# Decoder of a Trainium2 megakernel: the rows of maxima are sent by DMAs that ScalarE issues, not SyncE

## The reference

```python
qkv = x @ Wi.T + bi
scores = einsum('bhqd,bhkd->bhqk', q, k) / sqrt(HD) + mask      # causal + alibi
attn = softmax(scores, axis=-1)
out = einsum('bhqk,bhkd->bhqd', attn, v)
x = x + out @ Wo.T + bo
x = x + gelu(layer_norm(x) @ W1.T + b1) @ W2.T + b2
```

## Time and profile before

| what | value |
|---|---|
| runs, median (lowest, highest) | 3368.85 us (3360.95, 3370.55), n = 3 |
| the profiled execution, its own time | 3376.56 us |
| its span; granted clock | 3374.8 us; 0.841 |
| decoder's second pass, first to last exponential | about 158 to 1608 us of the span |
| DMA issues of rows of maxima | 192, all by SyncE, 4 KB each |

### The profile page before, as it was taken

One profiled execution on the slowest core, in us unless ns is written; L12 is line 12 of the kernel. 1 busy time (PEld: TensorE's weight loads), 2 busy tenths in 40 slices (PEclk: granted clock), 3 DMA queues, 4 the chain that ended last, 5 costly groups with the idle time before them and its releaser, 6 DMA issues. The chain is left out here.

```text
span 3374.8 us, 38611 instructions
## 1 busy us (share of the span) xinstructions
PE 2632.2 (78%) x12745; PEld 1113.1 (33%) x12745; DVE 1938.5 (57%) x4374; ACT 1426.5 (42%) x2500; POOL 580.1 (17%) x595
## 2 busy tenths in 40 slices
PE   6489898979979798998676898862566695888847
PEld 4233333333424233332232344330222342222225
DVE  2376666656757565774255723348999524766243
ACT  2155555545646554666243032333333242355510
POOL 1100111110101111100055001004878201000000
PEclk7599988988979897999678998875888797798978
DMA  2211212120211212110100000000000002110010
GB/s 69 87 64 42 81 39 77 48 87 30 77 55 68 73 39 77 38 57 24 40 1 6 1 0 23 0 13 0 0 0 0 25 0 87 40 38 31 14 76 13
DMA packets 64218, 129.88 MB, mean 38 GB/s; under 512 B 18698, under 2 KB 34442, under 8 KB 60334
## 3 DMA queue, kind: packets, MB, share of 16 engines
q1 hardware_dynamic: 64020, 127.42, 10.7%
HBM read 92.30 MB, written 34.08 MB: 37 GB/s over the span
## 5 line engine op out<-in xcount | busy, mean ns | idle before, releaser
L1432 ACT ACTIVATE sb_prob<-ps 128x512 f32<-128x512 f32 (+1 forms) x1216 | 651.8, 575 | 545.3 <-PE ps L1243 407.0
L1243 PE MATMUL ps<-sb_q_stack_half,sb_k_stack_half 81*128 81x512 bf16 (+2 forms) x1792 | 482.9, 326 | 150.8 <-DMA sb_q_stack_half<-sb_max_rows 100.0
L1217 PE MATMUL ps<-sb_k_stack_half,sb_q_stack_half 78*128 78x512 bf16 (+3 forms) x1536 | 493.2, 356 | 42.2 <-DMA sb_q_stack_half<-alibi 26.6
L1353 DVE TENSOR_REDUCE sb_row_max<-ps 128x1 f32<-128x512 f32 x512 | 347.3, 687 | 239.9 <-PE ps L1217 238.1
L1362 DVE CUSTOM_DVE_ANT_0 sb_masked_scores<-ps,sb_mask_row 128x128 bf16<-128x128 f32 (+3 forms) x512 | 228.6, 488 | 184.5 <-PE ps L1217 183.9
L1362 DVE CUSTOM_DVE_ANT_0 sb_masked_scores<-ps,sb_mask_row,sb_row_max 128x128 bf16<-128x128 f32 (+3 forms) x512 | 274.2, 545 | 105.0 <-PE ps L1217 101.6
L1243 PEld LDWEIGHTS ps<-sb_q_stack_half,sb_k_stack_half 81*128 81x128 bf16 x1792 | 166.2, 101 | 441.2 <-ACT sb_prob L1432 149.6
L1264 PE MATMUL ps<-sb_prob,sb_v_first_half 128*9 128x512 f32 (+3 forms) x2048 | 256.1, 575 | 0.0
L624 DVE CUSTOM_DVE_ANT_0 sb_masked_scores<-ps,sb_mask_row 128x128 f32<-128x128 f32 (+7 forms) x256 | 183.5, 756 | 107.7 <-PE ps L553 106.5
L2557 POOL TENSOR_TENSOR sb_inflow<-sb_delta_u,sb_b_spread 128x1024 f32<-128x1024 f32 x64 | 233.2, 3668 | 45.9 <-ACT sb_b_spread L2540 45.9
L1217 PEld LDWEIGHTS ps<-sb_k_stack_half,sb_q_stack_half 78*128 78x128 bf16 x1536 | 154.4, 105 | 216.9 <-DVE sb_row_max L1362 54.7
(11 more groups left out here) (407 smaller groups left out, 4266.8 us busy)
## 6 DMA issues: line engine op xcount, KB each, us to landing
sb_q_stack_half<-q_rows SPq DMA_DIRECT2D x192, 96.0 KB
sb_k_stack_half<-k_rows SPq DMA_DIRECT2D x96, 192.0 KB
o_rows<-sb_o_raw SPq DMA_DIRECT2D x64, 256.0 KB, 6.6
sb_k_stack_half<-k_rows SPq DMA_DIRECT2D x96, 96.0 KB
q_rows<-sb_qk_parts SPq DMA_DIRECT2D x48, 128.0 KB, 2.1
k_rows<-sb_qk_parts SPq DMA_DIRECT2D x48, 128.0 KB, 2.2
sb_k_stack<-k_parts SPq DMA_DIRECT2D x24, 192.0 KB
sb_q_stack<-q_parts SPq DMA_DIRECT2D x8, 576.0 KB
```

The costliest lines, as they stand in the source:

```text
L1217: pe.matmul(M.ps[:, k % RING, 0:hi - lo], qst[half][0:S1_ROWS, s, j, at:at + P], kst[half][0:S1_ROWS, s, lo // CH, j, 0:hi - lo], start=Tr ...
L1243: mm = pe.matmul(bank[:, x * w + lo:x * w + hi], kst[half][0:S2_ROWS, s, t // 4, j, t % 4 * P:(t % 4 + 1) * P], qst[half][0:S2_ROWS, s, j, ...
L1353: dve.reduce_max(rowmax[:, tau % 3, 0, at:at + 1], M.ps[:, k % RING, 0:w], AX_X).then_inc(first_done, 1)
L1432: act.activation(prob[:, st % PROB_STEPS, heads[0]:heads[-1] + 1, a:CH], scores.rearrange("p (j q) -> p j q", j=len(heads)), ACT.Exp).then ...
```

## The change

SyncE's `max_rows` and its duty are taken out. ScalarE gets a function of the same name, which waits for its own turn to be written and issues the same three DMAs, and calls it behind the instruction of the unit that follows the turn. Where the step has no second pass (the head of the pipeline, task 0 alone) it is called right behind the turn.

```diff
--- before.py
+++ after.py
@@ -1005,7 +1005,6 @@
         duty = {}
         for tau in range(self.NT):
             l, b, half, g = self.tasks[tau]
-            duty.setdefault(self.turn_step[tau] + 1, []).append((0, "rows", tau))
             saved = self.last_core
             if tau + 1 < self.NT:
                 saved = self.step_of[(tau + 1, 1)]
@@ -1107,15 +1106,6 @@
 
             @block.sync
             def _(sp):
-                def max_rows(tau):
-                    l, b, half, g = tasks[tau]
-                    s = plan.slot[tau]
-                    sp.wait_ge(unit_done, plan.turn_unit[tau] + 1)
-                    for part in range(3):
-                        row = S1_ROWS + part
-                        sp.dma_start(qst[half][row:row + 1, s, :, :].rearrange("o j (i q) -> o (j i) q", i=4),
-                                     turned[ROWS * part:ROWS * (part + 1), tau % 2, :]).then_inc(rows_in[half][s], 16)
-
                 def o_rows(tau):
                     c, g = divmod(tau, NGRP)
                     p = c % 2
@@ -1186,9 +1176,7 @@
                 sp.wait_ge(aux_in, 16 * sum(HALF_SLOTS))
                 for s in range(len(plan.duties)):
                     for _, what, x in plan.duties[s]:
-                        if what == "rows":
-                            max_rows(x)
-                        elif what == "out":
+                        if what == "out":
                             o_rows(x)
                         elif what == "heads":
                             heads(x)
@@ -1422,6 +1410,14 @@
                     act.activation(turned[:, tau % 2, :], M.ps[0:3 * ROWS, S2_BANK + v % RING, 0:P],
                                    ACT.Copy).then_inc(unit_done, 1)
 
+                def max_rows(tau):
+                    half, s = tasks[tau][2], plan.slot[tau]
+                    act.wait_ge(unit_done, plan.turn_unit[tau] + 1)
+                    for part in range(3):
+                        row = S1_ROWS + part
+                        act.dma_start(qst[half][row:row + 1, s, :, :].rearrange("o j (i q) -> o (j i) q", i=4),
+                                      turned[ROWS * part:ROWS * (part + 1), tau % 2, :]).then_inc(rows_in[half][s], 16)
+
                 def weight(v, tau, t, heads):
                     st = plan.step_index[(tau, t)]
                     a, w, diag = place(tau, t)
@@ -1470,13 +1466,19 @@
                         act.wait_ge(rest_ready, u + 1)
                         act.activation(parts[:, u % 2, 1, :], full[:, u % 2, :], ACT.Copy).then_inc(mid_ready, 1)
 
-                before = None
+                before, late = None, None
                 for s, step in enumerate(steps):
                     for x, (kind, tau, heads, _) in enumerate(step["units"]):
                         if kind == "turn":
                             turn(step["units_at"] + x, tau)
                         else:
                             weight(step["units_at"] + x, tau, step["t"], heads)
+                        if late is not None:
+                            max_rows(late)
+                        late = tau if kind == "turn" else None
+                        if late is not None and step["task"] is None:
+                            max_rows(late)
+                            late = None
                         if x == 0:
                             for done in plan.saves.get(s, ()):
                                 save(done)
```

## The result

The changed kernel takes 3271.07 us in the median of four runs (3265.23 to 3290.47). The kernel before took 3364.9 us on the same chip (3352.83 to 3370.55): ratio 0.9736, 95% interval 0.9686 to 0.9786. Five runs more gave 0.9719 [0.9694, 0.9743]. So it is 2.6 to 2.8% faster, some 94 us, where the prediction had 3296 in a range of 3262 to 3345. The profiled execution took 3265.23 us, 111 less than the profiled one of before (3376.56).

The account below looks back on a forecast made before the run. The decoder was taken as TensorE-bound with holes, the largest being waits for the maxima's transfers. Terms -72.1 - 0.9 - 20 + 20 = -73 us gave 3296 us for the median, in a range of 3262 to 3345.

Parts of the forecast that it names:

- rival of the recovered head: Decoder's start: TensorE's 27 us wait ahead of 153.25 is won back as well, giving 3269 us; chance 0.06.
- a sign of being wrong: Decoder's span shorter by more than 85 us would show that the wait at the head was recovered.
- The five waits: TensorE's waits for the maxima's transfers at tasks 20, 28, 36, 44, 52 vanish: 72.1 us less.
- task 12: TensorE's wait of 0.87 us ahead of 377.17, for the maxima's transfers, goes too: 0.9 us less.
- Rows behind the loads: Rival: at the five tasks rows still land behind the stack loads; gain 62 instead of 72 us, 3306; chance 0.12.
- The head: Decoder's start: TensorE's 27.02 us wait counted as no gain, since ScalarE waits for the query parts; bounds 0 and 4.
- ScalarE's price: 192 issues moved to ScalarE delay its next instructions by 1.3 us a turn: 20 us more, bounds 5 and 83.
- The two bad kinds of turn: Turns like task 20 (second exponential follows) pass on about 1.0 us, like task 17 (gelu behind) 1.25 us.
- each other turn: Remaining turns of a period of eight pass on 0.2 us or less of ScalarE's delay to TensorE.
- The clock: TensorE's 0.50 clock behind the five waits, 79.7 us of busy time, mostly recovers: 20 us less, bounds 0 and 27.
- SyncE's queue: SyncE loses its row issues and waits for turns; what stands behind them gains 0, at best 26.6 us.

Follow-up runs that it names:

- Run 3: The kernel before, with only task 0's rows issued by ScalarE and all others by SyncE; 3361.65 us, ratio 0.9989.
- Run 4: The kernel before, with ScalarE issuing only the rows of the seven tasks 12, 20, ... 60; 3269.59 us, ratio 0.9701.
- run 5: The kernel before, SyncE issuing all rows, with the four stack loads of a first half spread over four later steps; 3266.21 us, ratio 0.9695.
- Run 7: The changed kernel with each of the three DMAs split in two of 8 rows, 384 issues in place of 192; 3389.16 us, ratio 1.0057.
- run 1: The changed kernel measured again, unaltered, as a scale for the others; 3278.03 us, ratio 0.9719 to the kernel before.
- Run 6: run 5 with the load of each eighth task put ahead of the reciprocals on SyncE; 3269.34 us, ratio 0.9712.
- run 8: The changed kernel with the rows issued right behind the turn, ahead of the next exponential; 3295.4 us, ratio 0.9786.

## Why the prediction was right

Its main mechanism held, and the measured time lies within its range. But two numbers look like its rival of the recovered head: the measured 3271 is nearer to that rival's 3269 than to the forecast's 3296, and the decoder became 97 us shorter, where over 85 was named as the mark of the rival and a sign of being wrong. Run 3 rules the head out. The rest came from terms that were each somewhat off the same way, and that the number is so near to 3269 is chance.

**The five waits (-72.1, and -0.9 for task 12): right.** No wait for the maxima is left. Runs 4 and 5 show that these waits, and nothing else of the 192 issues, are the gain.

**Rows behind the loads (62 instead of 72): wrong as a rival, half right as a fact.** The rows are not held back to the loads' end. Task 20 alone can't show it: in order of issue they would have come 5.9 us behind their last issue (549 - 543.1), and they took 5.0. Task 17 can, whose rows are issued beside two stack loads in both kernels; the three issues and their landing, before and after:

```profile
L1116 SPq DMA_DIRECT2D sb_q_stack_half<-sb_max_rows x3: 591/591/777, 487.3 to 488.8; - x3
...
DMA to landing us min/median/max: 2.3/2.4/15.1
```

```profile
L1418 ACTq DMA_DIRECT2D sb_q_stack_half<-sb_max_rows x3: 526/617/687, 474.4 to 475.6; - x3
...
DMA to landing us min/median/max: 2.3/2.5/5.2
```

15.1 us became 5.2. The pair isn't quite alike: before, all 14 DMAs of the two loads were issued ahead of the rows, after the change 11 to 13 of them. But in order of issue that would make little difference. Before, the loads' first issue and the rows' last landing are 27 us apart (476.98 to 503.92); 11/14 of this from 466.56 on is 488, and the rows had landed at 480.7, while packets of the loads went on until 493. Run 4 has both in one kernel: task 17, still with SyncE, 15.4 us, and task 20, with ScalarE, 5.0. The Trainium skill (DMA: Bandwidth & Descriptors, Issuing engines are not separate DMA queues) says that starting DMAs from several engines saves only the time to issue them. Here it saved more: a small transfer on ScalarE's queue isn't kept behind the loads on SyncE's. It is not free of them either, 5.2 us at task 17 and 5.7 at task 20 where the median of all is 2.2. Only a few of its packets are late: of the 48 packets of 256 bytes in task 20's rows, 39 had moved 0.8 to 0.9 us behind the last issue in both kernels, and the last nine started 9.2 to 9.4 us behind it before (562.12 to 562.37) and 1.9 to 4.2 us behind it after the change (535.95 to 538.28). The prediction's working put the landing at 545.3, 2.2 us behind the last issue (a median that counts from an issue's start), with 3.9 us to spare; in truth 5.0 us passed and 1.8 us was to spare.

**The head (0): right.** Run 3 shows it, ratio 0.9989, within the prediction's bounds of 0 and 4 us.

**ScalarE's price (+20): right in kind, a little high.** The waits grew by 13.8 us; TensorE's idle time in the decoder fell by 56 us where -73 + 20 = -53 was forecast. The two bad kinds of turn were as foretold, in place and nearly in size: behind the gelu TensorE waits 4.3 us instead of 2.90, 1.4 more where 1.25 was said, and at task 20's kind 0.7 to 1.1 where 1.0 was said. What was too high is the 0.2 or less for each other turn: they added next to nothing. Run 7 shows how little room is left: three issues more added 70 us of waits.

**The clock (-20, bounds 0 and -27): right in its direction, a little small, and read from one execution.** TensorE's busy time in the decoder fell by 41 us in the profiles (37 against run 1's), and its part at 0.50 from 238 to 140 us. But busy time at the lower clock isn't a constant of the kernel. Run 3, in which the five waits stand, had only 172.9 us of it and 1246.3 us busy; run 4, in which they are gone, 172.7 and 1245.7. In the 25 us behind each of the five waits it is 79.8 us in the profile of before, the 79.7 that the prediction built on, but 22.7 in run 3 with the same waits and 20.4 in the changed kernel. So neither that row nor the two profiles can size this term.

Two estimates can, roughly. The medians: 94 us less, of which 56 is idle time and some 7 the part behind the decoder, leave 31; with run 1's 88.6 us it is 26. And the granted clock of every execution: the time at 0.50, 2 x (1 - clock) x span, averages 1044 us over the 17 executions of the kernel before that stand beside run 1 and 903 over nine of the changed kernel, 142 less. In the traces 52 of this is idle time and some 20 is busy time behind the decoder; the other 70, at the prediction's own rate (79.7 to 52.3), are 24 us. So the term is 24 to 31 us by estimate, where 20 was taken. Whether its bound of 27 held stays open.

**SyncE's queue (0): right.** Alibi 28.0 against 26.6, the normed heads 5.2 against 6.4. Run 6 shows why there is no cheap gain in it: SyncE serves both, and what is put first makes the other late.

**The sum.** Idle -56 against -53, busy -41 against -20 in the profiles, and about 14 us outside the decoder that nobody had forecast: 111 against 73. By the medians it is 89 to 94 against 73, and the missing 16 to 21 us are 3 in the waits, 4 to 11 in the clock, by the estimates above, and some 7 behind the decoder.

## What to carry to other kernels

When a small transfer on the critical path is late, look first at what its issuing engine has queued ahead of it: spreading four bulk loads over later steps (run 5) gave the same 3% as moving the small one to another engine, without its price on ScalarE, but with 4 to 5 us more of waits for the loads. If it moves to a busy engine, put its issues beside an instruction that runs anyway and move only those that are late: three issues a turn cost 13.8 us of waits in all, nearly all of it at 13 of 64 turns, six issues cost 83, and a place one instruction earlier cost some 17 us of time. And a wait that the trace names is worth nothing if another wait ends at the same time; ask what stands behind it, as at the head. Last, don't size a clock term from one trace: behind the same five waits, busy time at the lower clock was 79.8 us in one execution and 22.7 in another.

## What was not expected of the hardware

A DMA of 4 KB issued by ScalarE landed in at most 5.7 us while loads of SyncE were under way (6.2 in run 8), where SyncE's own needed up to 16.2; at tasks 17 and 20 it was the last nine of 48 packets that were late in either kernel. Issues on ScalarE run beside an activation that has started, but hold up the next: 0.608 us each, 0.627 for one of half the size, so between 4 and 2 KB the size makes no difference. And the short waits of run 7, 80 in place of 44, went with a lower clock as the long ones had: 1.7 us on average, (162.7 - 28.8)/79, with a mean granted clock of 0.849 over ten executions against 0.862.
